# Issuing all seven clears of the sorted rows in the first batch of the plain attention

## The reference, cut to what matters

```python
xn = _layernorm(x, axis=-1)                      # x: (8, 512, 256), float32
x = x + _L0_attn_ref(xn, Wq, Wk, Wv, Wo) + _L0_ffn_ref(xn, ...)

def _L0_ffn_ref(src, ...):                       # plain attention, 16 heads of 16
    x = _layer_norm(src + attn, ln1_g, ln1_b)
    expert_idx = remainder(floor(x @ router_w + router_b), 4)
    for e in range(4):                           # FF of 1024
        y = relu(x @ W1[e] + b1[e]) @ W2[e] + b2[e]
        ff_out = ff_out + where(expert_idx == e, y, 0)
    return _layer_norm(x + ff_out, ln2_g, ln2_b)
```

## Time and profile before

| | |
|---|---|
| median of 3 runs | 2013.69 us (2011.32 to 2016.56) |
| the profiled execution | 2005.31 us |
| its span in the trace | 2003.5 us |
| granted TensorE clock, mean | 0.952 of full speed |
| busy: PE, DVE, POOL, ACT | 1782.1, 1306.4, 980.4, 829.6 us |

### The profile page before, as it was taken

The page is one execution under the profiler, slowest core; times in us unless marked ns, Lnnn a source line. Parts: engine busy times, 40 slices in busy tenths (PEclk is TensorE's granted clock), DMA queues, the critical chain, the costliest instruction groups (busy, mean ns, idle before and its releaser), DMA issues.

```text
span 2003.5 us, 32159 instructions
## 1 busy us (share of the span) xinstructions
PE 1782.1 (89%) x11513; PEld 1056.6 (53%) x11514; DVE 1306.4 (65%) x2934; ACT 829.6 (41%) x1140; POOL 980.4 (49%) x631
## 2 busy tenths in 40 slices
PE   4889889889877299996589999999999999999998
PEld 2333333333333199996454655546556475564654
DVE  5776777777777367775765765657656576565761
ACT  2555545545544044443244252442534425334152
POOL 1134343443454334444537377374773746737464
PEclk7899999999989699998789999999999999999999
DMA  7548437537552645553300100101001010010000
GB/s 113 65 125 163 57 110 132 91 110 131 87 181 95 234 155 215 214 216 125 90 1 1 43 1 6 37 2 43 1 3 41 1 43 1 1 43 2 24 10 11
DMA packets 81440, 151.52 MB, mean 76 GB/s; under 512 B 11638, under 2 KB 55318, under 8 KB 75420
## 3 DMA queue, kind: packets, MB, share of 16 engines
q1 hardware_dynamic: 77980, 141.12, 27.1%
q0 software_dynamic: 3072, 8.39, 1.2%
q10 hardware_dynamic: 256, 0.26, 0.1%
HBM read 84.47 MB, written 39.85 MB: 62 GB/s over the span
## 4 chain that ended last, share of the span: by engine, by line
PE 44%; DVE 3%; POOL 3%; issue 1%; ACT 1%; DMA 0%; POOLq 0%; DVEq 0%; SPq 0%
PE a_psO L729 12%; PE a_psS L715 11%; PE a_psO L752 6%; PE a_psM L689 5%; PE a_psS L677 4%; PE a_psS L661 4%; PE a_psS L742 3%; ACT a_probs L480 1%; POOL a_k_tok L362 1%; POOL a_q_tok L362 1%; DVE a_junk L546 1%; POOL a_oT L385 0%; DVE a_alibi L623 0%; DVE a_qL L536 0%; DVE a_probs L516 0%
## 5 line engine op out<-in xcount | busy, mean ns | idle before, releaser
L397 POOL TENSOR_TENSOR a_probs<-a_probs 128x1024 f32<-128x1024 f32 x144 | 341.6, 2399 | 300.0 <-PE a_psO L729 300.0
L546 DVE CUSTOM_DVE_ANT_0 a_junk<-a_psM,a_alibi 128x512 bf16<-128x512 f32 x512 | 333.3, 689 | 198.9 <-PE a_psM L689 196.4
L1334 DVE TENSOR_REDUCE f_n_tok<-f_psR 128x1 f32<-128x512 f32 x512 | 326.2, 681 | 132.2 <-PE f_psR L1518 131.3
L480 ACT ACTIVATE a_probs<-a_psS 128x1024 f32<-128x1024 f32 x256 | 248.9, 1024 | 271.5 <-PE a_psS L715 270.7
L1278 ACT ACTIVATE f_probs<-f_psS 128x1024 f32<-128x1024 f32 x256 | 247.9, 1023 | 225.9 <-PE f_psS L1537 215.8
L729 PE MATMUL a_psO<-a_probs,a_v 128*32 128x512 f32 x2048 | 244.0, 597 | 0.0
L1518 PE MATMUL f_psR<-f_kP,f_qP 48*128 48x512 f32 x512 | 171.4, 524 | 66.4 <-DVE f_n_tok L1334 47.0
L1518 PEld LDWEIGHTS f_psR<-f_kP,f_qP 48*128 48x128 f32 x512 | 66.2, 194 | 251.9 <-DVE f_n_tok L1334 119.1
L689 PE MATMUL a_psM<-a_kH,a_qH 64*128 64x512 f32 x512 | 122.8, 475 | 29.1 <-DVE a_n_tok L546 29.1
L1550 PE MATMUL f_psO<-f_probs,f_v 128*32 128x512 f32 x1024 | 143.2, 632 | 1.6 <-ACT f_oT L1271 0.9
L752 PE MATMUL a_psO<-a_wo,a_oT 128*128 128x256 f32 x512 | 127.7, 396 | 4.4 <-POOL a_oT L385 4.4
(11 more groups left out here) (211 smaller groups left out, 3524.9 us busy)
## 6 DMA issues: line engine op xcount, KB each, us to landing
w_w_high<-w_parts SPq DMA_DIRECT2D x23, 1024.0 KB, 5.3
w_w_low<-w_parts SPq DMA_DIRECT2D x23, 1024.0 KB, 7.3
sorted_rows<-f_zeros SPq DMA_DIRECT2D x6, 1408.0 KB, 7.9
f_kP<-f_high SPq DMA_DIRECT2D x64, 128.0 KB, 5.9
f_qP<-f_high SPq DMA_DIRECT2D x64, 128.0 KB, 7.6
f_w_raw<-in_L_ffn_W SPq DMA_DIRECT2D x16, 512.0 KB, 7.7
w_parts<-f_w_high SPq DMA_DIRECT2D x16, 512.0 KB, 6.6
w_parts<-f_w_low SPq DMA_DIRECT2D x16, 512.0 KB, 7.4
```

The lines of the kernel that those rows point to most:

```text
L397: nc.gpsimd.tensor_tensor(slots, slots, probs[:, first - GRP:first - GRP + 2, :], ALU.add).then_inc(added.sem, 1)
L480: nc.scalar.activation(probs[:, slots, :], psS[:, 2 * p:2 * p + 2, :], ACT.Exp).then_inc(exp_done.sem, 1)
L546: nc.vector.tensor_tensor_reduce(out=junk[:, a, :], in0=psM[:, a, :], in1=alibi[:, h, :], scale=1.0, scalar=-3.0e38, op0=ALU.add, op1=ALU.max,
L1334: nc.vector.tensor_reduce(n_tok[:, c, column:column + 1], psR[:, ring_bank("max", batch, u), :], AX.X, ALU.max, negate=True).then_inc(max_ ...
```

## The change

`clear_rows` is called for all seven parts in batch 0, at the place of the first call before, and not in later batches.

```diff
                     load_chunk(n)
                     if i == 0 and b + 2 < B:
                         load_rows(b + 1)
-                    if i == 0:
-                        clear_rows(b)
+                    if b == 0 and i == 0:
+                        for n in range(B - 1):
+                            clear_rows(n)
```

## The result

| | before | changed |
|---|---|---|
| median of 20 runs | 2009.82 us (1991.86 to 2017.10) | 2016.03 us (2007.82 to 2020.39) |
| ratio | | 1.0038, 95% interval 1.0019 to 1.0056 |
| profiled execution | 2005.31 us | 2015.36 us |

The change makes the kernel slower, by 0.38% or 7.6 us (the ratio is taken over all runs; the two medians alone differ by 6.2 us).

What follows compares the result with a forecast made beforehand. PE, busy 89% of the span, was taken to bound the kernel. Terms 14.8 + 2.5 - 5 = +12.3 us made 2005.3 into 2017.6 profiled and the three-run median 2013.7 into 2026; 8-in-10 range 2014 to 2038 us.

Steps and rivals of the forecast that it cites:

- term 3: Batches 1 to 6: without their clears, small transfers of maxima delay PE less; -5 us, bounds nothing to 9.6 us given back.
- The queue's order and the burst's rate: SP's queue in batch 0: transfers land in issue order, clears move at 387 GB/s, so the last lands at 132.9.
- SP is through at about 106.8: Batch 0: six more clear issues at about 0.55 us each, 3.3 us, hidden by SP's 7.1 us wait for POOL.
- Term 1: Batch 1's norm: late chunk 1 delays POOL's splits and power, so DVE and PE halt; +14.8 us, bounds 14.4 to 21.4.
- the small transfer inside the burst: Batch 0: maxima sent at 119.15 travel amid clears, about 2 us charged to PE and DVE, covered by the 14.8 us halt.
- Term 2: Batch 1, after PE's halt: granted clock falls to half for a while; +2.5 us, between 1.7 and 3.4.
- The base: Whole kernel: +12.3 us added to 2013.7, the median of three runs, giving 2026 us.
- The stores were held back: Batch 0, against a rival where stores and chunk 1 slip past the burst: -5 us, 2008.7 us, chance 0.11.
- the burst was not slow: Batch 0, against a rival where clears run at 296 GB/s with no give-back: +24.8 us, 2038 us, chance 0.14.
- ACT's queue was not blocked: Batch 0, within the slow-burst rival (chance 0.14): maxima landing only with the last clear would add a second clock pause, 1.7 us.
- A small net loss: Whole kernel, rival: full give-back, low ends of the other terms, PE catching up; about +5 us, 2019 us, chance 0.13.

Runs made afterwards that it cites:

- the second trace of before: The kernel before, unchanged, run and traced again as a null comparison: ratio 1.0000 (0.9979 to 1.0022), traced execution 2008.6 us.
- the experiment that has nothing else: Kernel before, still one clear per batch, but issued only after the next batch's first maxima have landed: 1998.54 against 2007.15 us, ratio 0.9962.
- the second trace of the changed kernel: The changed kernel, unchanged, measured and traced again: 2016.59 us against 2007.15 us for the kernel before, ratio 1.0058 (1.0040 to 1.0077).
- splits later: Changed kernel with POOL's splits of chunks 1 and 2 moved from the end of batch 0 into batch 1: 2000.85 against 2004.97 us for before, ratio 0.9975.
- late in batch 0: Kernel before with all seven clears issued in batch 0, but behind the load of chunk 2: 1998.83 against 2004.97 us, ratio 0.9979.

## Why the prediction came out as it did

The direction, the place and the mechanism held; the size was too large against the first measurement (+12.3 us forecast, 7.6 measured, 3.8 to 11.3) and about right against the second (11.6). The step that failed is term 3, what batches 1 to 6 give back: -5 us forecast, 8.2 to 9.8 in the traces.

- **The queue's order and the burst's rate** held: 386 to 387 GB/s from 110 to 122 us, and the clears ahead of the stores. By the prediction the last clear lands at 132.9 and chunk 1 at 137.4; by the view of the transfers the last clear, issued at 122.71, landed at 134.5, and POOL started on chunk 1 at 139.53.
- **"SP is through at about 106.8"** was wrong. Seven issues took 23.8 us; from the third on one takes about 4 us, near the 3.7 us that 1408 KB need at 387 GB/s, so it looks as if the queue took a new one only as an earlier one drained. The stores were issued at 127.17 instead of 110.08 and landed 8.9 and 8.2 us later, where some 25 had been forecast. As the order is kept, this changed chunk 1 little; it comes 2.0 us later than forecast.
- **Term 1, +14.8 us:** measured +16.8 and +17.0 at L128 in the two traces of the changed kernel, against the first trace of before, and 15.1 and 15.2 against the second. L128 stands at 153.74 where 151.7 was forecast, and these 2 us are chunk 1's. From 126 to 134 us the engines moved 342 to 374 GB/s instead of 387, which fits most of them; whether the slow issues did it no run separates. The wait of DVE itself is 11.0 and 13.4 us, since DVE came later too, by the small transfer inside the burst and the clock; the first was foreseen as covered, and both are.
- **Term 2, +2.5 us:** the delay grows from 16.8 to 19.6 us behind the halt, +2.8, and by 2.7 against the second trace of before. PE lost 2.7 us there by the sum of the clock used above.
- **Term 3, -5 us: the step that failed.** I let the three long waits of the earlier trace rows fall to the mean of the others, 0.8 us, and left the others alone. They fall to nothing, and so do two shorter ones whose clears I had left out. The nearest row was there: the earlier trace rows, a small transfer issued beside stores and a chunk but with no clear, for which PE does not wait. The waits alone are 7.2 us in the first trace of before; the whole give-back is 8.2 to 9.8 us in the four pairs of traces and 7.6 us (4.8 to 10.2) in the experiment that has nothing else. With -9, the middle of the four, my sum would have been +8.3. Its upper bound, 9.6, was about right (the terms named for it add up to 9.5).
- **The base.** Added to the median of three runs the forecast became 2026; against the median of 20, 2009.8, that is 0.8% where 0.61% was meant. The 2026 itself lies 10 us above the measured 2016.03, and the high base is 3.9 of them; that three runs gave such a base is chance. A mean of the two measured ratios, 1.0048, is +9.6 us.
- **The rivals.** The stores were held back, the burst was not slow, and ACT's queue was not blocked: the transfer sent at 122.95 amid the burst made PE wait 1.73 us, and in the second trace the one at 121.07 not at all. "A small net loss" had the right size for the first measurement, and for a part of its reason, the full give-back.

The timeline of PE in the changed kernel, at the two small transfers of batch 0 that meet the burst:

```profile
108.18 1.22 PE L1538 MATMUL f_psS<-f_qP,f_kP 64*128 64x512 f32 x4 [2.20 <-DMA f_qP<-f_n_row]
...
129.57 0.73 PE L1538 MATMUL f_psS<-f_qP,f_kP 64*128 64x512 f32 x4 [1.73 <-DMA f_qP<-f_n_row]
```

What stays open is the remainder of the give-back beyond the waits (0 to 2 us against the first trace of before, where they are 7.2; some 4 to 5 against the second, where they are 5.1). Shorter dips of the clock where PE no longer waits would explain it, but the dips differ too much from one trace to the next to tell. In two places the working read its rows loosely: the wait of 1.45 us named with the earlier trace rows stands in the timeline of PE and not there, and the three runs lie within 0.14% of their median, not 0.13.

## What to carry to other kernels

In this kernel, bulk work without a deadline was cheap only at places with nothing urgent behind it, in its own queue or, on the same engines, in another: the same 9.7 MB cost 17 us ahead of a load that an in-order engine waits for, and no time clear of the noise 18 us later (4.2 us gained, against 7.6 with no burst at all). Price a move of such work by two questions: what stands behind it in the queue and how much slack that has, and which small transfer it was delaying where it stood. Here the second question led to the better kernel: an order behind the small transfer, 0.38% faster than before.

## What the runs showed of the hardware

An issue on SP was no longer short with several large transfers ahead of it: seven clears of 1408 and 1024 KB took 23.8 us to issue (11.5 us for four, 30.7 us for seven behind other transfers), where one took 0.55. The view of the transfers of the changed kernel, from 102.9 to 125 us, shows that a clear then lands 12.7 us after its issue began. With issues about 4 us apart, some three were under way at once, which is an estimate from these two numbers:

```profile
sorted_rows<-f_zeros SPq DMA_DIRECT2D x6, 1408.0 KB, 12.7
sorted_rows<-f_zeros SPq DMA_DIRECT2D x1, 1024.0 KB, 11.8
```

A transfer of 4 KB on ACT's queue passed through a burst on SP's and didn't wait for its end: where PE waited for it, it was 1.5 to 2.2 us, 0.4 to 1.9 us more than in the traces of before at the same place; in three cases PE didn't wait (the transfers sent at 121.07 in the second trace of the changed kernel, at 123.29 in "splits later" and at 122.09 in "late in batch 0"). Its issue on ACT amid the burst took up to 1.8 us instead of 1.2; before, an issue at 50.6 us, beside the moves of q and k, took 1.8 too. The stretches of the changed kernel behind the first small wait and behind the halt (length, busy PE, PEld, DVE, ACT, POOL, clock, DMA share, GB/s):

```profile
106.00:110.00 4.00, 1.82 (x8) 0.73 (x12) 1.22 (x3) 0.98 (x2) 2.47 (x2) 0.70 1.09 379
110.00:114.00 4.00, 3.64 (x16) 1.33 (x8) 1.97 (x4) 1.54 (x3) 0.94 (x1) 0.50 1.09 387
114.00:118.00 4.00, 3.64 (x14) 0.91 (x15) 3.05 (x6) 1.94 (x2) 1.27 (x1) 0.50 1.09 386
...
156.00:158.00 2.00, 1.29 (x4) 0.86 (x5) 2.00 (x5) 0.00 (x0) 0.00 (x0) 0.50 0.00 0
158.00:160.00 2.00, 2.00 (x11) 1.49 (x9) 0.45 (x1) 1.15 (x2) 0.00 (x0) 0.50 0.00 0
160.00:162.00 2.00, 2.00 (x14) 0.52 (x10) 1.29 (x2) 1.43 (x3) 0.00 (x0) 0.50 0.00 0
```

A wait of 2.2 us at 106 to 108 was followed by some 12 us at half clock (1.2 in place of 2.4 GHz), the halt of 11.6 us by about 6. During the halt PE stood still from about 145 us, and the granted clock fell only between 148 and 150. The length of the low stretch doesn't follow that of the pause here: behind 107 us PE lost 6.2 us of busy time in this trace, and in the nine others between 1.4 and 11.
